# Landing pauses among the row scatters, and another start of the expert stage

## What is computed

```
x = x + xattn(ctx, layernorm(x), mask)     # 128-wide heads' work: 4 heads of 64, 1024 queries per batch,
                                           # keys: the batch's own 1024 rows and 77 context rows
x = x + ffn(layernorm(x))                  # routing to 64 experts

# ffn: scores = sigmoid(x @ gate_w.T); the best 4 of 8 groups, in them the best 8 experts per token
pos = position of (token, k) among those that chose the same expert, in token order
valid = pos < 256                          # an expert takes its first 256 tokens, later ones are dropped
buf[e, pos] = x[token]                     # rows gathered by expert
y = (silu(buf @ w_gate) * (buf @ w_up)) @ w_down
out[token] += y[e, pos] * weight           # 8 experts add into one row
```

## Time and profile before

| | us |
|---|---|
| median of three runs | 1108.94 |
| the profiled execution | 1109.89 |
| its span in the trace | 1108.1 |
| scatters of rows (line 1080), first to last start | 257.8 to 813.3 |
| additions of the expert stage (line 1155), first to last start | 828.13 to 1065.63 |
| POOL busy, share of the span | 616.9, 56% |
| PE busy, share of the span | 892.2, 81% |

### The profile page before, as it was taken

The page is one execution under the profiler, slowest core; times in us unless marked ns, Lnnn a source line. Parts: engine busy times, 40 slices in busy tenths (PEclk is TensorE's granted clock), DMA queues, the critical chain, the costliest instruction groups (busy, mean ns, idle before and its releaser), DMA issues.

```text
span 1108.1 us, 13512 instructions
## 1 busy us (share of the span) xinstructions
PE 892.2 (81%) x3944; PEld 636.7 (57%) x3944; DVE 661.7 (60%) x1953; ACT 463.1 (42%) x931; POOL 616.9 (56%) x571
## 2 busy tenths in 40 slices
PE   2869999989999999998999987895149999888200
PEld 1446666646666656666655545784038888777100
DVE  4485638986598886597876666756514443333106
ACT  2834675743756634757443433432013333222000
POOL 4540232303785653675564673566638888888840
PEclk9979999999999999999998996987569999999755
DMA  6829801111211322210126312100739999888689
GB/s 241 303 52 386 315 1 41 39 41 63 102 68 69 124 90 64 97 57 7 65 83 228 107 35 93 34 28 18 256 126 288 314 275 164 163 156 130 71 256 392
DMA packets 85336, 150.79 MB, mean 136 GB/s; under 512 B 14089, under 2 KB 53049, under 8 KB 83215
## 3 DMA queue, kind: packets, MB, share of 16 engines
q1 hardware_dynamic: 54543, 112.32, 29.3%
q0 software_dynamic: 30720, 37.61, 17.0%
HBM read 69.19 MB, written 97.45 MB: 150 GB/s over the span
## 4 chain that ended last, share of the span: by engine, by line
PE 57%; DVE 14%; issue 10%; DMA 7%; POOL 6%; ACT 5%; another core or an unknown queue 1%; POOLq 0%; SPq 0%; DVEq 0%; ACTq 0%
PE ps_o L1313 17%; PE ps_u L1377 5%; PE ps_s L1289 5%; PE ps_s L1291 5%; PE ps_u L1233 4%; PE ps_u L1203 4%; POOL sum L1155 3%; DMA sum<-again,row_ids 2%; PE ps_u L1325 2%; PE ps_o L1308 2%; PE ps_o L1386 2%; DVE mp L1648 2%; DMA out_rows<-again,row_ids 2%; POOL out_rows L1155 2%; DMA again<-out_rows 2%
## 5 line engine op out<-in xcount | busy, mean ns | idle before, releaser
L1080 POOL DMA_INDIRECT slot_rows<-rows,slot_idx x256 | 253.7, 991 | 199.4 <-issue 94.4
L1648 DVE TENSOR_REDUCE mp<-ps_u 128x1 f32<-128x512 f32 x256 | 164.8, 685 | 93.0 <-PE ps_u L1233 78.7
L1518 ACT ACTIVATE probs<-ps_s 128x512 f32<-128x512 f32 x256 | 139.6, 596 | 153.7 <-PE ps_s L1291 107.9
L1155 POOL DMA_INDIRECT sum<-again,row_ids x84 | 131.1, 1561 | 26.0 <-issue 22.3
L1313 PE MATMUL ps_o<-probs,pool 128*128 128x512 f32 (+1 forms) x288 | 137.8, 601 | 4.3 <-ACT den L1539 4.3
L1377 PE MATMUL ps_u<-again 128*128 128x256 f32 x512 | 123.2, 384 | 0.0
L1313 PE MATMUL ps_o<-probs,V 128*128 128x512 f32 (+1 forms) x216 | 105.4, 610 | 5.7 <-ACT probs L1521 3.8
L1820 DVE TENSOR_SCALAR again<-ps_o,again 128x256 f32<-128x256 f32 x128 | 56.0, 479 | 77.7 <-DMA sum<-again,row_ids 50.0
L1291 PE MATMUL ps_s<-qbT,Kb 65*128 65x512 f32 (+1 forms) x252 | 102.1, 405 | 0.0
L1377 PEld LDWEIGHTS ps_u<-again 128*128 128x128 f32 x512 | 94.0, 194 | 10.6
L1155 POOL DMA_INDIRECT out_rows<-again,row_ids x44 | 68.8, 1564 | 27.0 <-DVE row_ids L1821 15.1
(11 more groups left out here) (201 smaller groups left out, 1761.9 us busy)
## 6 DMA issues: line engine op xcount, KB each, us to landing
again<-in_wexp SPq DMA_DIRECT2D x64, 384.0 KB, 6.3
slot_rows<-rows SPq DMA_DIRECT2D x2, 10272.0 KB, 35.1
again<-slot_rows SPq DMA_DIRECT2D x64, 321.0 KB
sum<-rows SPq DMA_DIRECT2D x2, 4352.0 KB, 27.9
again<-sum SPq DMA_DIRECT2D x8, 1024.0 KB, 11.3
Kb<-K SPq DMA_DIRECT2D x16, 275.5 KB
pool<-in_x SPq DMA_DIRECT2D x4, 1024.0 KB, 5.2
xres<-in_x SPq DMA_DIRECT2D x8, 512.0 KB
```

What stands on the lines that cost most here:

```text
L1080: pool.indirect_dma_start(out=slot_rows, out_offset=bass.IndirectOffsetOnAxis(ap=slot_idx[x][:, q, k:k + 1], axis=0), in_=rows[x][:, q, :] ...
L1155: pool.indirect_dma_start(out=(out, *sums)[e % PLANES], out_offset=bass.IndirectOffsetOnAxis(ap=row_ids[:, e % RING, t:t + 1], axis=0), in ...
L1518: act.activation(probs[:, n % NPR, hh, :], ps_s[:, u % NSC, :], ACT.Exp).then_inc(s["probs_made"], 1)
L1648: v.tensor_reduce(mp[:, i, tile, half:half + 1], bank((*t, i))[:, :], AX.X, ALU.max).then_inc(s["emptied_vec"], 1)
```

## The change

It has three parts.

1. GROUP becomes a table by half. In halves (2, 0) and (2, 1) each sixth scatter now waits for the landing of all the half's scatters before it, beside the pacing by values, which stays. In (3, 0) it is each fourth in place of each eighth, and in (3, 1) each fourth in place of none. The waiting scatters are 135, 141, 147, 153 and 159; 167, 173, 179, 185 and 191; then 197, 201, 205 and so on up to 221; and 229, 233 and so on up to 253. Half (2, 0) thus gets 5 pauses and half (2, 1) 5; half (3, 0) has 7 (before 3), half (3, 1) 7.
2. In the expert stage the first expert's down product goes ahead of the turning of expert 2 and the gate_up of expert 1, on PE, and its weigh ahead of hidden(1), on DVE. In weigh the copy of row_ids goes first, ahead of the wait for the product, and y_made counts tiles in place of experts, so that POOL may issue the first of an expert's two DMAs after the first of the two multiplications.
3. The DMAs of experts 1 and 2, which are the first on the two scratch planes, write plainly and don't add (4 of 128 DMAs).

```diff
-GROUP = 8
+GROUP = {(B - 2, 0): 6, (B - 2, 1): 6, (B - 1, 0): 4, (B - 1, 1): 4}
...
     def grouped(self, b, x):
-        return (B - 2, 0) <= (b, x) < (B - 1, 1) and self.paced(b, x, 0, 0) is None
+        return (b, x) in GROUP
...
-                sp.wait_ge(s["y_made"], e - RING + 1)
+                sp.wait_ge(s["y_made"], 2 * (e - RING + 1))
...
-                if plan.grouped(b, x) and before and before % GROUP == 0:
+                if plan.grouped(b, x) and before and before % GROUP[(b, x)] == 0:
                     pool.wait_ge(s[f"scattered{x}"], HALF_SCATTERS * b + 16 * before)
...
             for e in range(E):
-                pool.wait_ge(s["y_made"], e + 1)
                 if e >= PLANES:
                     pool.wait_ge(s[f"added{e % PLANES}"], 32 * (e // PLANES))
                 for t in range(2):
-                    pool.indirect_dma_start(
-                        out=(out, *sums)[e % PLANES],
...
+                    pool.wait_ge(s["y_made"], 2 * e + t + 1)
+                    at = bass.IndirectOffsetOnAxis(ap=row_ids[:, e % RING, t:t + 1], axis=0)
+                    if 0 < e < PLANES:
+                        i = pool.indirect_dma_start(
+                            out=sums[e - 1], out_offset=at, in_=y_out[e % RING][:, t, :], in_offset=None,
+                            bounds_check=NTOK + DUMP - 1, oob_is_err=False)
+                    else:
+                        i = pool.indirect_dma_start(
+                            out=(out, *sums)[e % PLANES], out_offset=at, in_=y_out[e % RING][:, t, :], in_offset=None,
+                            bounds_check=NTOK + DUMP - 1, oob_is_err=True, compute_op=ALU.add)
+                    i.then_inc(s[f"added{e % PLANES}"], 16)
...
                 if e >= 2:
-                    pe.wait_ge(s["y_made"], e - 1)
+                    pe.wait_ge(s["y_made"], 2 * (e - 1))
...
             gate_up(0)
+            down(0)
             for e in range(1, E):
                 if e < E - 1:
                     turn(e + 1)
                 gate_up(e)
-                down(e - 1)
+                if e > 1:
+                    down(e - 1)
...
             def weigh(e):
                 r = e % RING
+                if e >= RING:
+                    v.wait_ge(s[f"added{(e - RING) % PLANES}"], 32 * ((e - RING) // PLANES + 1))
+                v.wait_ge(s[f"x_in{r}"], 16 * (e // RING + 1))
+                link(v.tensor_copy(row_ids[:, r, :].unsqueeze(2), xr[r][:, :, D:D + 1]))
                 v.wait_ge(s["y_full"], e + 1)
-                if e >= RING:
-                    v.wait_ge(s[f"added{(e - RING) % PLANES}"], 32 * ((e - RING) // PLANES + 1))
                 for t in range(2):
-                    v.tensor_scalar(y_out[r][:, t, :], ps_y[:, e % 2, t, :], xr[r][:, t, D + 1 + e:D + 2 + e], None, ALU.mult)
-                v.tensor_copy(row_ids[:, r, :].unsqueeze(2), xr[r][:, :, D:D + 1]).then_inc(s["y_made"], 1)
+                    v.tensor_scalar(y_out[r][:, t, :], ps_y[:, e % 2, t, :], xr[r][:, t, D + 1 + e:D + 2 + e], None, ALU.mult
+                                    ).then_inc(s["y_made"], 1)
             hidden(0)
+            weigh(0)
             for e in range(1, E):
                 hidden(e)
-                weigh(e - 1)
+                if e > 1:
+                    weigh(e - 1)
```

More of the change, by code:

```diff
@@ L1154, in _ @@
                 for t in range(2):
-                    pool.indirect_dma_start(
-                        out=(out, *sums)[e % PLANES],
-                        out_offset=bass.IndirectOffsetOnAxis(ap=row_ids[:, e % RING, t:t + 1], axis=0),
-                        in_=y_out[e % RING][:, t, :], in_offset=None, bounds_check=NTOK + DUMP - 1, oob_is_err=True,
-                        compute_op=ALU.add).then_inc(s[f"added{e % PLANES}"], 16)
+                    pool.wait_ge(s["y_made"], 2 * e + t + 1)
[9 more added lines that the diff above has]
+                    i.then_inc(s[f"added{e % PLANES}"], 16)
         @block.tensor
@@ L1814, in weigh @@
                 r = e % RING
-                v.wait_ge(s["y_full"], e + 1)
                 if e >= RING:
                     v.wait_ge(s[f"added{(e - RING) % PLANES}"], 32 * ((e - RING) // PLANES + 1))
+                v.wait_ge(s[f"x_in{r}"], 16 * (e // RING + 1))
+                link(v.tensor_copy(row_ids[:, r, :].unsqueeze(2), xr[r][:, :, D:D + 1]))
+                v.wait_ge(s["y_full"], e + 1)
                 for t in range(2):
-                    v.tensor_scalar(y_out[r][:, t, :], ps_y[:, e % 2, t, :], xr[r][:, t, D + 1 + e:D + 2 + e], None, ALU.mult)
-                v.tensor_copy(row_ids[:, r, :].unsqueeze(2), xr[r][:, :, D:D + 1]).then_inc(s["y_made"], 1)
+                    v.tensor_scalar(y_out[r][:, t, :], ps_y[:, e % 2, t, :], xr[r][:, t, D + 1 + e:D + 2 + e], None, ALU.mult
+                                    ).then_inc(s["y_made"], 1)
             hidden(0)
+            weigh(0)
             for e in range(1, E):
                 hidden(e)
-                weigh(e - 1)
+                if e > 1:
+                    weigh(e - 1)
             weigh(E - 1)
```

## The result

The changed kernel took 1119.8 us in the median of 6 runs (1118.35 to 1122.61), the kernel before beside it 1111.05. The ratio is 1.0082, with a 95% interval of 1.0053 to 1.0111. The forecast was 1111, and a difference too small to tell from none. It was wrong: the change cost 5.9 to 12.3 us here, and 1119.8 lies at the very end of the stated range, 1101 to 1120. The profiled execution took 1122.61, with a span of 1120.9 where the one before had 1108.1.

The account below looks back on a forecast made before the run. POOL was taken to bound the kernel, through its scatters and then the expert stage. Scatters +3.7 and expert stage -1.5 gave +2.2: 1112.1 against the profiled execution, or 1111 against the median, range 1101 to 1120.

Parts of the forecast that it names:

- What bounds: Scatters and expert stage: the last scatter sets the stage's start; POOL, at 3.74 per expert against PE's 3.03, bounds the stage.
- The residual's additions: POOL, batch 3: those of (3, 0) come some 2 to 3 later behind pauses, costed at nothing.
- The calm pause: POOL's scatters: each new pause costs between 1.68 and 1.88 without heavy loads, taken as 1.75.
- The load on top of a pause: Batch 2 and (3, 1): up to three pauses each fall into weight loads, at 0 to 2.1; 1 each taken.
- The relief: PE and DVE before scatter 193: shorter runs credited with 4 at 710.95, putting number 193 at 707.
- The first rival: Scatters: pauses only cost, 193 stays at 710.95; +6.2 to +7.5, 1115 to 1116.5, or 1120 with full load price; chance 0.3.
- +3.7: Scatter chain on POOL: the last scatter, number 256, starts at 817.0 in place of 813.28.
- The expert stage: After the last scatter: expert 3 begins on POOL at 837.9 in place of 839.4, a gain of 1.5.
- The lead of 0.1 to 0.4 for loading hid: Expert stage, PE: estimated time for loading hid ahead of the first down product, which takes 0.86.

Follow-up runs that it names:

- The late burst: Changed kernel with the third burst's 17 weight loads issued only after the last scatter landed and the first experts' rows were loaded; 1119.61 in a single run.
- the sixes: Against the kernel before: new expert stage, pauses at each sixth scatter in batch 2, batch 3 as before; 1107.21, ratio 0.9924; again 1103.31, ratio 0.9922.
- The second timing of the change: The changed kernel itself once more, on another chip beside the kernel before; 1120.57, ratio 1.0035.
- the stage alone: Against the kernel before: only the new expert stage, with the scatters' pauses as they were; 1115.97, ratio 0.9986.
- The delays: Changed kernel with two writes to POOL's own memory in place of each wait for a landing; 1130.42, ratio 1.0116 to the kernel before.
- three in flight: Changed kernel with each scatter waiting for the landing of the one three before it, in place of the pauses; 1133.32, ratio 1.0138 to the kernel before.

## Why the prediction was wrong

The forecast had the last scatter at 817.0, and it started at 827.03. Of the 10.0 between them, 2.4 lie ahead of the first new pause, 1.3 between 132 and 193, and 6.4 behind 193.

**What bounds: right.** The last scatter sets the start of the expert stage, and from number 193 on POOL waits for no data. The residual's additions, queued behind the pauses of (3, 0), were costed at nothing. DVE did stand for them, 7.60 until 737.58, but the choice for (3, 1) still lay ready at 758.53, 7.6 before POOL came.

**The calm pause: right.** 1.75 over the 0.30 was taken; in (3, 1), past the burst, idle times of 237 to 249 are 1.91 to 2.20, or 1.6 to 1.9 over.

**The load on top of a pause: this is the step that failed.** I wrote "at 0 to 2.1 each. I take 1 each, 3 per batch". The bound came from one pause of 4.29 before [725.25, rows 6], and I called it one under heavy loads. It wasn't: the DMA share in it was 0.30 at 100 GB/s, against 0.98 at 333 GB/s ahead of 229 now. Beside the burst, 229 and 233 took 5.1 and 3.4 over the calm 1.9, or 8.5 where I had 3, and more than three times 2.1 would have given. In batch 2, numbers 135 and 173 took 3.1 and 1.2 over a calm 2.15, 4.3 for 3. The late burst shows the cause. From 193 to 256 it is 116.36 where I had 110.0; 5.5 of the 6.4 are this term. The stands ahead of 221 and 253 became 2.7, where they were 1.98 before, which I had not foreseen; that is 1.2 over the 1.75 that I had for each.

**The relief: there, larger than credited, and in the whole change worth as little as said.** I credited 4. From number 132 the choice for (3, 0) comes 9.85 earlier (98.04 after it in place of 107.89). But POOL was at 193 only 106.23 after 132, against the 104.9 of the forecast: 1.3 late, the size of what the loads of batch 2 cost over their 3. The first rival had the right time with its full price for the loads, 1120, and its sign too, as 193 started at 710.67. Its reason was wrong: the choice lay ready 8.2 before, so it was POOL that came late, and the sixes gain 8.8 where POOL still waits. The forecast's mechanism was right, with its load term mis-sized.

**What I did not ask** is which part of the relief is worth its price. I read the change as one sum, +3.7. It is a gain of some 9 in batch 2, a small loss in (3, 0) (1.9 in time, not told from nothing), and a loss of 8.6 (in time) to 12 (in the chain) in (3, 1), where the only things still to come from other engines are the last row writes. There POOL's stand of 5.19 ahead of number 241, in the kernel without the fours of (3, 1), goes to 2.00, and everything else is added. By the times the parts sum to between 0 and 2, and to between 4 and 6 with the 12 of the chain for (3, 1). The second timing of the change (ratio 1.0035, or 3.9) fits that; the first, 9.1, lies above it, and no run shows why.

**The expert stage: right in size, but not seen in the time.** I forecast -1.5, or 24.62 from the last scatter's start to expert 3, against 26.12 before. The two profiles of the change have 25.77 and 24.70, the stage alone has 24.64, and all thirteen profiles with the new stage lie between 24.23 and 26.39. The first addition comes 14.49 and 13.42 after the last scatter's start (forecast 13.57, before 14.85), the plain writes take 0.98 to 1.03, and the waits ahead of experts 1, 2 and 3 are there. The lead of 0.1 to 0.4 for loading hid was an estimate from no row; in the changed kernel that product ends 1.18 after DVE's hidden, where lead and product were to take 0.96 to 1.26. As time the stage can't be told from nothing (0.9986).

**The base.** Number 132 to 256 takes 211.2 in the profile of before and 218.6 in the stage alone, with the same pauses, while the two profiles of the change have 222.6 and 222.0, and those of the sixes alone 205.9 and 207.5. So part of the 11.4 is luck of the profile that I worked from, which had few of the long stands. The stage alone ran on another chip, and its profiled execution was the longest of its ten, so it isn't told apart how much lies with the execution and how much with the chip. The load term doesn't hang on this: it is read from 193 to 256 in the changed kernel alone.

**Open.** Why a gap on POOL lets ACT and DVE run. The delays show that no landing need be waited for, and three in flight that a steady stream of few is no help. But a gap of 2.75 is also longer than a calm landing of 2.1, so it isn't told apart whether it counts that POOL issues no DMA for a while (it writes memory in the delays, so it doesn't rest) or that nothing is in flight. A kernel with no pause at all, beside which three in flight should stand, was not run.

## What to carry to other kernels

Price a pause by who is waiting at that place: it gains only while the pausing engine would itself wait later for those that it relieves, and is plain cost behind the last such wait. Place it away from bursts of loads, or make it of a fixed length; here a wait for a landing grew from 1.9 to 7.06 with the loads beside it. When you take the price of a pause under load from one row, look at the DMA share in it first. And two profiles with the same pauses differed by 7 us over these 124 scatters, so take two before you compare chains.

## What the runs showed that I had not expected

- A landing of 128 rows of 321 numbers took 2.13 calm, and 7.28 and 5.45 with 17 loads of 384 KB on their way.
- With POOL's scatters in long runs, PE did 291 matmuls in the 90 us from 610 to 700 and ACT stood up to 9.19; with a gap at each sixth 374 and 380, at a granted clock of 0.96 and 0.98 in place of 0.91, and ACT's longest stand there that lacked a known releaser was 5.49 and 6.33.
- A gap made of two memory writes, 2.75 in all, gave most of the relief of a wait for the landing: the choice for (3, 0) came 101.05 after number 132, against 98.04 with the waits and 107.89 to 112.81 with no pauses in batch 2. A steady stream with at most three scatters in flight did not (110.19); that kernel took 1.4% more than the one before.
- A plain indirect write of 128 rows of 256 numbers took 0.98 to 1.03 on POOL, one that adds 1.56.
